# Six PSUM banks a head: every tile of nodes by two matmuls, and the sums moved out in two parts

## What is computed

```
seq    = (x @ W_seq).reshape(2048, 16, 32)
scores = leaky_relu(score1[:, :, None] + score2[:, None, :], 0.2)      # per head
attn   = softmax(scores + (1 - adj) * (-65500))
hidden = (attn @ seq per head).reshape(2048, 512) @ W_out + b_out
x      = layernorm(x + elu(hidden))
x      = layernorm(x + 1e-08 * (ones @ (dinv * (A + I) * dinv)) @ x)   # A from (adj + adj.T) / 2
```

## Time and profile before

| | us |
|---|---|
| median of 3 runs | 734.97 |
| lowest, highest | 733.68, 736.03 |
| the profiled execution's own time | 734.38 |
| its span (first to last instruction) | 732.6 |
| PE busy | 716.7 |
| DVE busy | 521.0 |
| ACT busy | 409.3 |
| mean granted TensorE clock | 0.998 |

### The profile page before, as it was taken

The page is one execution under the profiler, slowest core; times in us unless marked ns, Lnnn a source line. Parts: engine busy times, 40 slices in busy tenths (PEclk is TensorE's granted clock), DMA queues, the critical chain, the costliest instruction groups (busy, mean ns, idle before and its releaser), DMA issues.

```text
span 732.6 us, 23462 instructions
## 1 busy us (share of the span) xinstructions
PE 716.7 (98%) x10731; PEld 554.1 (76%) x10731; DVE 521.0 (71%) x872; ACT 409.3 (56%) x315; POOL 118.6 (16%) x146
## 2 busy tenths in 40 slices
PE   7999899999999999999999999999999999999996
PEld 5878899999999999999999995444444444444444
DVE  4568999999999999999999976878721110332332
ACT  1578998988988999899999933333321010000000
POOL 0200110001321212213000011744322000000000
PEclk9999999999999999999999999999999999999999
DMA  9994415113433344233121123994069400101101
GB/s 330 416 417 156 136 54 151 61 46 74 89 67 62 67 76 89 63 68 66 47 61 47 46 75 67 184 192 91 14 109 169 67 1 1 43 30 44 43 30 43
DMA packets 33351, 71.24 MB, mean 97 GB/s; under 512 B 3044, under 2 KB 14052, under 8 KB 31076
## 3 DMA queue, kind: packets, MB, share of 16 engines
q1 hardware_dynamic: 24736, 51.64, 20.1%
q0 software_dynamic: 8240, 17.84, 17.1%
q10 hardware_dynamic: 276, 0.26, 0.1%
HBM read 77.86 MB, written 8.65 MB: 118 GB/s over the span
## 4 chain that ended last, share of the span: by engine, by line
PE 87%; DMA 4%; issue 4%; DVE 2%; SPq 1%; POOL 1%; ACT 0%; POOLq 0%; DVEq 0%; ACTq 0%
PE bank L638 24%; PE bank L745 14%; PE bank L639 13%; PE bank L731 11%; PE bank L694 8%; PE bank L643 4%; PE bank L644 4%; PE bank L642 4%; PE bank L702 4%; DMA RZ<-in_L_gnn_W_seq_dram 2%; DMA RZ<-s_rows_dram 1%; SPq L347 1%; PE bank L686 1%; DMA s_rows_dram<-W 1%; DVE RZ L1087 1%
## 5 line engine op out<-in xcount | busy, mean ns | idle before, releaser
L638 PE MATMUL bank<-RP,RG 128*128 128x132 f16 (+1 forms) x3072 | 369.3, 222 | 2.5 <-DVE RG L1097 1.4
L639 PE MATMUL bank<-RP,MT 128*128 128x66 f16 (+1 forms) x3072 | 369.0, 195 | 0.0
L823 ACT ACTIVATE RZ<-RZ,TAB 128x2048 fp8e4<-128x2048 f32 x159 | 305.1, 1994 | 19.6 <-DVE RG L1097 16.6
L638 PEld LDWEIGHTS bank<-RP,RG 128*128 128x128 fp8e4 x3072 | 280.3, 97 | 3.2 <-DVE RG L1097 1.7
L639 PEld LDWEIGHTS bank<-RP,MT 128*128 128x128 fp8e4 x3072 | 281.0, 98 | 0.1
L643 PE MATMUL bank<-RP,RG 128*128 128x66 f16 (+1 forms) x1024 | 202.0, 197 | 0.0
L642 PE MATMUL bank<-RP,RG 128*128 128x66 f16 (+1 forms) x1024 | 199.4, 195 | 0.0
L644 PE MATMUL bank<-RP,MT 128*128 128x66 f16 (+1 forms) x1024 | 197.4, 193 | 0.0
L1087 DVE TENSOR_SCALAR RZ<-RZ,TAB 128x2048 int8<-128x2048 f32 x97 | 123.4, 1272 | 2.4 <-DMA RZ<-s_rows_dram 2.3
L745 PE MATMUL bank<-RZ,MT 128*128 128x512 f16 (+1 forms) x544 | 110.8, 367 | 0.0
L1097 DVE TENSOR_TENSOR RG<-RZ,MT 128x512 int32<-128x512 int32 x159 | 108.7, 684 | 0.0
(11 more groups left out here) (141 smaller groups left out, 718.6 us busy)
## 6 DMA issues: line engine op xcount, KB each, us to landing
RG<-in_adj_t_dram SPq DMA_DIRECT2D x16, 1024.0 KB, 8.3
RZ<-s_rows_dram SPq DMA_DIRECT2D x60, 256.0 KB, 3.3
seq_copy_dram<-SEQ SPq DMA_DIRECT2D x8, 528.0 KB, 5.4
RZ<-in_x_dram SPq DMA_DIRECT2D x16, 256.0 KB, 3.0
RP<-in_adj_p_dram POOLq DMA_DIRECT2D x8, 512.0 KB, 8.1
RP<-in_adj_tp_dram POOLq DMA_DIRECT2D x8, 512.0 KB, 12.5
out_dram<-W SPq DMA_DIRECT2D x16, 256.0 KB, 2.0
RQ<-in_x_t_dram SPq DMA_DIRECT2D x2, 1024.0 KB, 14.5
```

The source lines that it names most:

```text
L638: mm(bank[:, c:c + 4 * d], step, both, start=(j == 0 and i % IB == 0), **ends)
L639: last = mm(bank[:, c:c + 4 * d].rearrange("p (e c d) -> p e c d", e=2, c=2)[:, :, 1, :], mask, edge, start=False, **ends)
L823: A(Z8[:, m % NZ, :], S1B[u], ACT.Relu, bias=SK[:, h, j:j + 1], scale=STEEP, saturate=False).then_inc(z_ready, 1)
```

## The change

A head now has six banks (`NBH`): the first 12 tiles `i` (`WHOLE`) lie three to a bank in four of them, the front, and the last four lie two to a bank in two, the back. Head `h` starts at bank `6 h` modulo 8 (`place`), so head `h + 1` starts in the two banks that head `h` doesn't use, and the rest of its banks are the front banks of head `h`. All tiles are done by two matmuls, of 132 and 66 columns.

PE's order follows from that. In heads 1 to 15 it takes for the first four tiles `j` only the first 6 tiles `i` (`FIRST`), then waits for `front_free` of the head before, and then does the other 10 tiles `i` of these four `j`. For the last four `j` (`LAST` = 12) it takes first the 12 tiles of the front, signals `front_ps`, and then the four of the back. In head 0 the first part is 12 tiles of two `j`.

ACT copies the front sums of head `h - 1` behind tile 8 and the back sums behind tile 9, and makes the operands of the next head behind tile 10, where it was behind 8. DVE adds the front behind tile 8, the back behind 9, scales behind 10, divides behind 11, and makes the low operands behind 12, where it was 11. Where the front's banks run past bank 7 (heads 1, 5, 9 and 13) the front is moved out in two parts. The memset is gone. In odd heads DVE makes 5 step tiles, no longer 6, and ACT 11 (`OWN_B`). Behind the attention the first transposes stay in banks 0 and 1, the later ones go to banks 2 and 3, and the products to 0 and 1 (`turned`). The edge counts of head 2 are taken by part; that and the count of lone nodes keep their arithmetic.

```
-    IB = 4
-    NB = NT // IB
+    NBH, WHOLE = 6, 12
...
-    OWNS = ((0, 1, 4, 6, 9, 12, 14),) + (OWN,) * (H - 1)
+    FIRST = [(WHOLE, 2)] + [(NT - WHOLE + 2, 4)] * (H - 1)
+    LAST = 12
+    OWN_B = (1, 4, 7, 10, 13)
+    OWNS = ((0, 1, 4, 6, 9, 12, 14),) + tuple(OWN_B if h % 2 else OWN for h in range(1, H))
...
-    AT_PREP, AT_EVAC, AT_HIGH, AT_LOW, AT_HID = 4, 7, 8, 11, 13
-    AT_LOWS = 9
+    AT_PREP, AT_EVAC, AT_HIGH, AT_LOW, AT_HID = 4, 7, 10, 12, 13
+    AT_LOWS = 8
...
+        def place(h, i):
+            b, at = (i // 3, i % 3) if i < WHOLE else (WHOLE // 3 + (i - WHOLE) // 2, (i - WHOLE) % 2)
+            return (NBH * h + b) % 8, at
+        def fronts(h):
+            first = NBH * h % 8
+            return ((first, 2, 0), ((first + 2) % 8, 2, 6)) if first + 4 > 8 else ((first, 4, 0),)
+        def backs(h):
+            return (((NBH * h + 4) % 8, 2, WHOLE),)
...
                 if h >= 2:
-                    pe.wait_ge(banks_free, 2 * h - 2)
+                    pe.wait_ge(back_free, BACK[h - 1])
...
+                    for i in tiles:
+                        b, at = place(h, i)
+                        c = at * 4 * d
+                        step, mask = G8[:, s, i * P:(i + 1) * P], MT8[:, j, i * P:(i + 1) * P]
+                        mm(pb[b][:, c:c + 4 * d], step, both, start=(j == 0 and at == 0), stop=(j == NT - 1), skip_group_check=True)
+                        last = mm(pb[b][:, c:c + 4 * d].rearrange("p (e c d) -> p e c d", e=2, c=2)[:, :, 1, :], mask, edge,
+                                  start=False, stop=(j == NT - 1), skip_group_check=True)
+                    return last
+
+                first, upto = FIRST[h]
+                for j in range(upto):
                     pe.wait_ge(g_ready, h * NT + (j + 1))
...
+                    sums(j, range(first))
+                if h == 0:
+                    pe.wait_ge(seq_sb, 2 * NT)
+                else:
+                    pe.wait_ge(front_free, FRONT[h])
+                for j in range(upto):
+                    sums(j, range(first, NT)).then_inc(g_used, 1)
+                for j in range(upto, LAST):
+                    pe.wait_ge(g_ready, h * NT + (j + 1))
+                    sums(j, range(NT)).then_inc(g_used, 1)
...
+                for j in range(LAST, NT):
+                    pe.wait_ge(g_ready, h * NT + (j + 1))
+                    last = sums(j, range(WHOLE))
+                last.then_inc(front_ps, 1)
+                for j in range(LAST, NT):
+                    sums(j, range(WHOLE, NT)).then_inc(g_used, 1)
...
+            def front_lows(h):
+                sc.wait_ge(front_ps, h + 1)
                 if h >= 1:
                     sc.wait_ge(hid_done, h)
+                low_sums(h, fronts(h), front_low)
+
+            def back_lows(h):
+                sc.wait_ge(g_used, NG + (h + 1) * NT)
...
+                low_sums(h, backs(h), back_low)
...
+            def front_sums(h):
+                ve.wait_ge(front_low, FRONT[h + 1])
+                whole_sums(h, fronts(h), front_free)
+
+            def back_sums(h):
+                ve.wait_ge(back_low, BACK[h + 1])
...
-                own.mark(V.memset(TB[:, :, IB - 1, 0:DV], 0.0))
...
                 if h > 0 and j == AT_EVAC + 1:
-                    whole_sums(h - 1)
+                    front_sums(h - 1)
                 if h > 0 and j == AT_EVAC + 2:
+                    back_sums(h - 1)
+                if h > 0 and j == AT_EVAC + 3:
                     scale_sums(h - 1)
                     add_sums(h - 1)
```

More of the change, by code:

```diff
@@ L315, in gat_then_normalised_adjacency, with banks, of_tiles, turned @@
         DS = bass.ds
-        def wide(h, e):
-            d = DV + 1 if h == ROW_HEAD else DV
[L319 to L330, removed]
+        def place(h, i):
[6 more added lines that the diff above has]
+            return (((NBH * h + 4) % 8, 2, WHOLE),)
+        def banks(h, part, e):
+            d = DV + 1 if h == ROW_HEAD else DV
+            first, count, tile = part
+            k = 2 if tile == WHOLE else 3
+            return PS[:, first:first + count, 0:k * 4 * d].rearrange("p b (i e c) -> p b i e c", i=k, e=2)[:, :, :, e, :]
+        def of_tiles(m, part):
+            first, count, tile = part
+            k = 2 if tile == WHOLE else 3
+            return m[:, tile:tile + count * k, :].rearrange("p (b i) c -> p b i c", i=k)
+        copies = [2 if h == ROW_HEAD else 1 for h in range(H)]
+        FRONT = [sum(len(fronts(g)) * copies[g] for g in range(h)) for h in range(H + 1)]
+        BACK = [sum(copies[:h]) for h in range(H + 1)]
+        def turned(t, k):
+            return t if t < 2 and k < KC - 1 else 2 + t % 2
         def s1_row_there(engine, h):
@@ L624, in _, with sums @@
                 if h >= 2:
-                    pe.wait_ge(banks_free, 2 * h - 2)
-                for j in range(NT):
+                    pe.wait_ge(back_free, BACK[h - 1])
+                d = DV + 1 if h == ROW_HEAD else DV
+                def sums(j, tiles):
                     s = (h * NT + j) % NG
-                    pe.wait_ge(g_ready, h * NT + (j + 1))
[L629 to L645, removed]
@@ L1031, in degrees @@
-            def degrees(h):
-                r = ROW.rearrange("p (b i) -> p b i", i=IB)
+                    for part in parts:
+                        degrees(h, part)
+                for part in parts:
+                    for e in range(2 * DV // c):
+                        m = of_tiles(TB, part)[:, :, :, e * c:(e + 1) * c]
+                        V.tensor_tensor(m, m, banks(h, part, 0)[:, :, :, e * (c + 1):e * (c + 1) + c], ALU.add).then_inc(free, 1)
+            def front_sums(h):
+                ve.wait_ge(front_low, FRONT[h + 1])
+                whole_sums(h, fronts(h), front_free)
@@ L1036, in degrees @@
                 own.wait(ve)
-                V.tensor_tensor(r[:, :, 0:IB - 1], r[:, :, 0:IB - 1], wide(h, 0)[:, :, :, ones_f], ALU.subtract).then_inc(row_sb, 1)
-                V.tensor_tensor(r[:, :, IB - 1], r[:, :, IB - 1], narrow(h, 1, 2)[:, :, DV], ALU.subtract).then_inc(row_sb, 1)
+                own.mark(V.tensor_tensor(r, r, banks(h, part, 0)[:, :, :, ones_f:ones_f + 1], ALU.subtract))
+                own.wait(ve)
             def lone_nodes():
-                ve.wait_ge(row_sb, 2)
```

101 lines of the change are left out of this document (48 added, 53 removed).

## The result

| | before | changed |
|---|---|---|
| median of 16 runs each, us | 735.38 | 736.99 |
| lowest, highest | 733.55, 736.17 | 735.65, 739.31 |
| span of the profiled execution | 732.6 | 735.4 |
| mean granted TensorE clock | 0.998 | 0.993 |

The ratio is 1.0028 (95% interval 1.0019 to 1.0037): the change makes the kernel 0.3% slower, by 1.6 us in the medians and some 2 us by the ratio. The forecast was 734.8, a hair faster.

A forecast was written before the change was run, and what follows sets the result against it. PE was taken to bound the attention. -7.5 + 5.75 + 0.55 - 0.4 = -1.6 us, -1.8 with covered moments of DVE lateness, and +1.65 net for the clock gave -0.15 us: 734.8 us, range 731.4 to 737.4.

The forecast's parts named there:

- What bounds it: In the attention, PE sets the pace at 23.1 us a head; DVE is only 1.5% quicker.
- The slower rival: In the attention, PE's new wait ties PE, ACT and DVE in one loop, DVE's lead is lost: 742.6 us; chance 0.10.
- Term 1: PE's attention matmuls: each triple becomes a pair, 7.5 ns less each, -7.5 us in all.
- Rival 3: Attention matmuls: the triple's 5 ns excess stays with the new pairs, saving only 2.6 us: 739.7 us; chance 0.05.
- Term 2: In head 1, PE waits once for DVE's addition of head 0's front sums: +5.75 us.
- Term 3: In head 2, PE waits for DVE's addition of head 1's front, +0.55 us; vanishes if the clock falls.
- Term 4: Behind the attention, ACT copies the last front while PE does the back, cutting PE's idle time: -0.4 us.
- The clock: Behind head 1's pause PE's clock falls to its lower level once, costing 2.2 us, net +1.65.
- The sum: Whole kernel: -1.8 us without the clock, +1.65 for it, together -0.15 us, 734.8 us.

The follow-up runs named there:

- filled pause: The changed kernel with 180 matmuls of 66 columns put into PE's pause in head 1; 735.66 us, ratio 1.0014.
- relief alone: The kernel before, with only DVE making 5 step tiles and ACT 11 in odd heads; 734.74 us, ratio 0.9992.
- early sums: The changed kernel with front sums added behind tile 4 on DVE and copied behind tile 5 on ACT, instead of 8 and 8; 730.93 us, ratio 0.9950.
- early sums with triples: The kernel with early sums, but every fourth tile i done by three matmuls of 66 columns; 734.19 us, ratio 1.0000.

## Why the prediction was wrong

- **What bounds it** was right: PE in the attention before, and after, with DVE and ACT full and never late from head 3 on. The slower rival, a lead that isn't carried, didn't come.
- **Term 1, -7.5 us, is the step that failed.** The counts were right, the price of 7.5 ns was wrong: it came from the starts of the two forms in a mixed stream. The 88.2 ns for a pair was a mean over pairs of which every third stands behind a triple and is cheap for it (57.3 + 30.0, the others 58.6 + 30.0), and in a stream of pairs alone each takes 88.8. Four tiles therefore save 360.3 - 355.3 = 5.0 ns by that sum, and 4.5 by the heads. 1024 x 4.5 ns is -4.6 us, 2.9 us less. I had a check for the sum of the mixture (360.3 ns for four tiles), and took it for a check of its parts. The Trainium skill, page "TensorE: Matmul & The Clock Gate", section "Back-to-back issue gap", gave -2.6 by its formula for the gap of a single matmul; the measured value lies between. Rival 3, built on it, had the right mechanism and too large a size: part of the triple's excess stays with the pairs, 3.0 of its 7.5 ns and not 5.
- **Term 2, +5.75 us:** 5.65 from start to start, 5.46 of it idle. Right in size and place. What the forecast doesn't say is that 5.0 us of it hang on two numbers that place the addition on DVE and ACT.
- **Term 3, +0.55 us:** there when the clock holds, gone when it falls. Both as stated.
- **Term 4, -0.4 us:** 1.67 to 1.29, right.
- **The clock** fell, as forecast. Its price of 2.2 us was 2.7 in the profiled executions: the low stretch with work in it was 5.8 us and not 4.35. Net of term 3 that is 2.18 by the filled pause, for the forecast's 1.65. The medians of that kernel gain 0.3 to 1.0 us and don't show the whole of it; why is open. That the clock would fall was inferred from one fall, 3.9 us behind the end of work. That was thin: behind the last matmul of the twelve profiled executions the fall came after 2.0 to 5.1 us. All of these are shorter than the pause, so the conclusion stood.
- **The sum**, against the profiled execution before. PE's stretch: -4.3 (960 triples at 4.5 ns) + 5.6 (the pause less a matmul's usual 0.03) + 2.7 (the clock) - 0.2 (moments of lateness, the kernel with relief alone) = +3.8, measured +3.58. The 0.2 left over is no more than the price of a triple is uncertain by: the heads before, 23.04 against 22.74, give 4.7 ns. Behind the stretch -0.4. Ahead of it -0.3 (94.34 to 94.02), which is what head 0's 64 triples would save, but two executions of one kernel differ by 1.25 us there, so this agreement can be luck. Together +2.9, and the spans say +2.8. The medians say +1.6; the missing 1.2 us are unexplained. The error of term 1, 2.9 us, is by itself enough to turn the forecast of no change into the loss of the profiled execution; the rest of the errors, mostly the clock's 0.5, are small beside it.
- The Trainium skill's warning of pauses (same page, section "Why this matters for your kernels") agrees with the trace: the clock fell in both profiled pauses of 5.65 us and in that of 4.45.

## What to carry to other kernels

Fewer buffers between producer and consumer move a wait from one place to another: ask where the releasing step stands in its own engine's program, not only how long it takes. Here a change that saved 4.6 us of matmuls lost 7.7 us of PE's stretch by leaving that step four tiles too late on DVE, and two numbers turned a loss of 0.3% into a gain of 0.5%. Price a form of instruction by a run with another share of it, or by the sum over a whole period, not by the distance to the next start, which puts one instruction's cost on its neighbours. And where the clock falls in a pause of PE, count both: the pause itself (here 5.65 us), and what the slow stretch behind it costs (2.7).

## What the runs showed of the hardware

- The granted clock fell to the lower of its two levels 4.5, 4.4 and 4.2 us after PE's last matmul had ended, in the three profiled pauses of 5.65, 5.65 and 4.45 us, and the stretches at the lower level were 6.83, 6.83 and 3.41 us long. Pauses of 0.6 and 1.6 us left it alone.
- Behind the last matmul of the program the same fall came after 3.9 us in the kernel before, and anywhere from 2.0 (early sums) to 5.1 us (early sums with triples) over the twelve profiled executions. One fall doesn't give the delay.
- At the lower level a pair of 132 and 66 columns takes 165 ns to the next pair, for 88.8: less than twice.
- Over whole heads, a tile by three matmuls of 66 columns costs 4.5 ns more than by one of 132 and one of 66, though the distances between single starts say 7.5.
- A stream of only 66-column matmuls, one in 31 ns, had 7 us of pauses that no other engine's work explains; 13 of the 14 ended 1.2 to 1.5 us behind a packet of the instruction queue. That it waited for instructions is likely and not shown.
